# Norm steps and the gated output read from PSUM, transposes sharing banks, in a fused macaron layer

## The reference

```
x = x + 0.5 * ffn(layernorm(x))      # router argmax over 8 experts, hidden 512, relu
x = x + attention(layernorm(x))
x = x + 0.5 * ffn(layernorm(x))      # the same weights
```

```
q, k, v = silu(x @ Wq), silu(x @ Wk), silu(x @ Wv)
scores = (q k^T) * mask ; o = scores v + lam_q * (q @ kv) ; kv = lam_c * kv + (k * lam_k)^T v
o = (o - mean) * rsqrt(var + eps) * gamma + beta
out = o * sigmoid(x @ Wg1 @ Wg2) @ Wo
```

## Time and profile before

| | us |
|---|---|
| median of 3 runs | 478.96 (478.88 to 479.79) |
| profiled execution, its own time | 478.87 |
| its span | 476.9 |
| outside the span | 1.97 |
| DVE busy in the span | 333.1 (70%) |
| PE busy | 369.2 (77%) |
| POOL busy | 284.4 (60%) |

### The profile page before, as it was taken

One profiled execution on the slowest core, in us unless ns is written; L12 is line 12 of the kernel. 1 busy time (PEld: TensorE's weight loads), 2 busy tenths in 40 slices (PEclk: granted clock), 3 DMA queues, 4 the chain that ended last, 5 costly groups with the idle time before them and its releaser, 6 DMA issues.

```text
span 476.9 us, 10199 instructions
## 1 busy us (share of the span) xinstructions
PE 369.2 (77%) x2508; PEld 328.8 (69%) x2508; DVE 333.1 (70%) x957; ACT 195.3 (41%) x586; POOL 284.4 (60%) x292
## 2 busy tenths in 40 slices
PE   4967999999898683854859797885078999999940
PEld 4966889999786563643647677664068988999930
DVE  3593566444647999899968896989966568556520
ACT  2542744555363230515343526243035544555510
POOL 0007764737864769393875776670067776777771
PEclk9999999999999986796979897988568999999995
DMA  8627886887620000000110101010157774676610
GB/s 241 250 71 240 235 227 195 225 202 212 200 76 19 11 11 6 7 11 0 55 52 1 40 6 46 0 44 1 45 180 217 233 196 151 195 209 209 174 38 0
DMA packets 41303, 54.00 MB, mean 113 GB/s; under 512 B 6212, under 2 KB 25818, under 8 KB 40992
## 3 DMA queue, kind: packets, MB, share of 16 engines
q1 hardware_dynamic: 34496, 39.49, 26.8%
q0 software_dynamic: 6176, 13.26, 11.2%
q10 hardware_dynamic: 576, 0.62, 0.5%
HBM read 41.93 MB, written 12.32 MB: 114 GB/s over the span
## 4 chain that ended last, share of the span: by engine, by line
PE 40%; DVE 19%; issue 16%; POOL 16%; DMA 3%; ACT 2%; DVEq 1%; POOLq 0%; ACTq 0%
PE bank L1232 14%; PE bank L1222 13%; POOL outer_all L298 5%; POOL rows L401 4%; PE bank L1184 3%; PE bank L1282 3%; PE bank L1178 3%; PE bank L1316 2%; DVE st L716 2%; PE bank L1214 2%; POOL qS L458 2%; DMA const_sb<-in_const 1%; POOL out_x L420 1%; ACT o_n L541 1%; DVE hT_b L940 1%
## 5 line engine op out<-in xcount | busy, mean ns | idle before, releaser
L387 POOL DMA_INDIRECT ring<-rows_d,token_in x92 | 88.0, 957 | 99.1 <-DVE token_in L900 72.3
L1222 PE MATMUL bank<-slot_xT,w_ring 128*128 128x128 f32 x736 | 103.2, 282 | 6.1 <-DVE hT_b L940 5.3
L1222 PEld LDWEIGHTS bank<-slot_xT,w_ring 128*128 128x128 f32 x736 | 93.1, 196 | 9.4 <-DVE hT_b L940 7.3
L940 DVE TENSOR_SCALAR hT_b<-bank,b_cur 128x128 f32<-128x128 f32 x184 | 55.9, 345 | 38.3 <-PE bank L1222 31.1
L1282 PE MATMUL bank<-outer_all,decay_sb 128*128 128x256 f32 x256 | 72.8, 412 | 12.0 <-POOL outer_all L298 8.1
L1282 PEld LDWEIGHTS bank<-outer_all,decay_sb 128*128 128x128 f32 x256 | 50.6, 207 | 29.2 <-issue 9.1
L298 POOL TENSOR_TENSOR outer_all<-qkv 128x512 f32<-128x512 f32 x60 | 63.4, 1084 | 1.7 <-ACT qkv L610 1.6
L1232 PE MATMUL bank<-w_sb,hT_a 128*128 x368 | 60.5, 288 | 3.7 <-issue 0.7
L572 ACT ACTIVATE hT_a<-bank,b_cur 128x128 f32<-128x128 f32 x184 | 57.5, 364 | 12.2 <-PE bank L1222 11.3
L1232 PE MATMUL bank<-w_sb,hT_b 128*128 x368 | 56.8, 277 | 0.0
L991 DVE TENSOR_REDUCE o_in<-qS 128x64 f32<-128x256 f32 (+1 forms) x64 | 53.6, 856 | 3.5 <-POOL qS L458 3.5
(11 more groups left out here) (127 smaller groups left out, 579.6 us busy)
## 6 DMA issues: line engine op xcount, KB each, us to landing
w_ring<-in_w1t SPq DMA_DIRECT2D x92, 256.0 KB
rows_d<-rows SPq DMA_DIRECT2D x8, 512.0 KB, 3.0
y_d<-y_sb SPq DMA_DIRECT2D x46, 64.0 KB
rows<-in_x SPq DMA_DIRECT2D x8, 256.0 KB, 7.8
w_sb<-in_w2t SPq DMA_DIRECT2D x1, 2048.0 KB, 9.4
rows_d<-rows SPq DMA_DIRECT2D x8, 256.0 KB, 2.3
ring<-rows_d,token_in POOLq DMA_INDIRECT x92, 4.1
decay_sb<-in_decay SPq DMA_DIRECT2D x1, 1024.0 KB
```

Of the source, the lines that this page charges most:

```text
L387: pool.indirect_dma_start(n_in_ring(G) if layer_of(G) == 0 else in_ring(G), None, rows_d[u], bass.IndirectOffsetOnAxis(ap=token_in[u][:, j ...
L940: last = nc.vector.tensor_scalar(hT_b[G % 2][:, f * P:(f + 1) * P], bank_b[:, f * P:(f + 1) * P], b1_cur[G % 2][:, 2 + f:3 + f], 0.0, ALU. ...
L1222: last = mm(to[:, f * P:(f + 1) * P], w1_ring[G % W1_BUFS][:, (2 * half + f) * P:(2 * half + f + 1) * P], slot_xT[G % 2][:, :], start=True ...
```

## The change

The norm's small steps keep `mean2`, `var` and `tt` in the last columns of PSUM bank 5 instead of in SBUF, and are written so that no step has more than one input in SBUF. That takes one step more (`SMALL` is 12, i = 0 to 12) and 17 instructions instead of 14. `output_copy` writes its result back into bank 3, and `gate` reads it there. To free bank 5, the transpose of xn goes to bank 3 and the transpose of q to bank 6, with the waits that go with it. `front` moves ahead of the last two `sum_d`, and on ScalarE `gate_tanh` ahead of `route_copy`. `y_bank` is bank 7 in the first layer and stays bank 6 in the second.

```diff
-        mean2, var, yy, tt, uu = (sb(n, [P, LN_W]) for n in ("mean2", "var", "yy", "tt", "uu"))
+        spread2, gap, yy, uu = (sb(n, [P, LN_W]) for n in ("spread2", "gap", "yy", "uu"))
+        ln_bank = bank[5]
+        mean2, var, tt = (ln_bank[:, 512 - (i + 1) * LN_W:512 - i * LN_W] for i in range(3))
...
-        SMALL = 11
+        SMALL = 12
...
-                nc.scalar.activation(o_nT[:, :], bank[3][:, :], ACT.Identity, bias=gb_sb[:, 1:2],
+                nc.scalar.activation(bank[3][:, :], bank[3][:, :], ACT.Identity, bias=gb_sb[:, 1:2],
...
                 if i == 0:
-                    nc.vector.tensor_tensor(mean2[:, c], st[:, c, 1], st[:, c, 4], ALU.add)
-                    stt(out=var[:, c], in0=st[:, c, 2], scalar=D * EPS, in1=st[:, c, 5], op0=ALU.add, op1=ALU.add)
-                    ins = nc.vector.tensor_tensor(tt[:, c], st[:, c, 1], st[:, c, 4], ALU.subtract)
+                    nc.vector.tensor_reduce(var[:, c], st[:, c, 2::3], AX_X, ALU.add)
+                    ins = nc.vector.tensor_reduce(mean2[:, c], st[:, c, 1::3], AX_X, ALU.add)
                 elif i == 1:
-                    ins = nc.vector.tensor_tensor(uu[:, c], tt[:, c], tt[:, c], ALU.mult)
+                    nc.vector.tensor_scalar(spread2[:, c], var[:, c], D * EPS, None, ALU.add)
+                    stt(out=gap[:, c], in0=st[:, c, 1], scalar=2.0, in1=mean2[:, c], op0=ALU.mult, op1=ALU.subtract)
+                    ins = stt(out=tt[:, c], in0=st[:, c, 1], scalar=2.0, in1=mean2[:, c], op0=ALU.mult, op1=ALU.subtract)
...
                 elif i == 10:
+                    ins = stt(out=tt[:, c], in0=tt[:, c], scalar=-10 / 8 / ROOT_3_8, in1=uu[:, c], op0=ALU.add, op1=ALU.mult)
+                elif i == 11:
                     ins = stt(out=rstd[par][:, c], in0=tt[:, c], scalar=15 / 8, in1=yy[:, c], op0=ALU.add, op1=ALU.mult)
...
-                nc.vector.scalar_tensor_tensor(out=o_gT[:, :], in0=gateT[s.par][:, :], scalar=1.0, in1=o_nT[:, :],
+                nc.vector.scalar_tensor_tensor(out=o_gT[:, :], in0=gateT[s.par][:, :], scalar=1.0, in1=bank[3][:, :],
...
+                        if h == PAIRS - 2 and k + 1 < STEPS:
+                            front(step(k + 1))
                         sum_d(here, h)
-                if k + 1 < STEPS:
-                    front(step(k + 1))
...
             def carry_product(s):
                 pe.wait_ge(kd_done, s.n + 1)
-                pe.wait_ge(gate_done, s.n + 1)
+                pe.wait_ge(qdT_done, s.n + 2)
...
             def q_transpose(s):
                 pe.wait_ge(qkv_done, BATCH * (s.n + 1))
-                transpose4(bank[5], lambda b: qkv[s.par][:, b * 3 * D:b * 3 * D + D], qT_ready)
+                wait(pe, gate_done, s.n)
+                transpose4(bank[6], lambda b: qkv[s.par][:, b * 3 * D:b * 3 * D + D], qT_ready)
```

More of the change, by code:

```diff
@@ L273, in build @@
         ROUTE_TURN = SPLIT[1][0] - 1 + 3
-        xT_bank, bank_a, bank_b, y_bank = bank[0], bank[1], bank[2], bank[6]
+        xT_bank, bank_a, bank_b = bank[0], bank[1], bank[2]
+        y_bank = [bank[7], bank[6]]
         counts_bank = bank[5]
-        router_bank = [bank[4], bank[7]]
-        SMALL = 11
+        router_bank = [bank[4], bank[6]]
+        SMALL = 12
         halved_by = lambda n, h: sum(helped(m, j) for m in range(n + 1) for j in range(PAIRS) if (m, j) <= (n, h))
@@ L587, in attn_front @@
                 wait(act, gate_ready, s.n - 1)
-                nc.scalar.activation(xnT[s.par][:, :], bank[5][:, :], ACT.Copy).then_inc(xnT_copied, 1)
+                nc.scalar.activation(xnT[s.par][:, :], bank[3][:, :], ACT.Copy).then_inc(xnT_copied, 1)
                 if s.n >= 2:
@@ L604, in copy_first_xn @@
                 act.wait_ge(xnT_ready, 1)
-                nc.scalar.activation(xnT[0][:, :], bank[5][:, :], ACT.Copy).then_inc(xnT_copied, 1)
+                nc.scalar.activation(xnT[0][:, :], bank[3][:, :], ACT.Copy).then_inc(xnT_copied, 1)
             def first_qkv(first):
@@ L657, in attention @@
                     age_carry(k - 1)
+                if k >= 0:
+                    gate_tanh(step(k))
                 if 0 <= k - 3:
@@ L660, in attention @@
                 if k >= 0:
-                    gate_tanh(step(k))
                     act.wait_ge(ln_ready, ln_turn(k) + 1)
@@ L735, in small @@
                 elif i == 3:
+                    ins = stt(out=var[:, c], in0=spread2[:, c], scalar=4.0 / D, in1=tt[:, c], op0=ALU.mult, op1=ALU.add)
+                elif i == 4:
                     ins = nc.vector.tensor_scalar(yy[:, c].bitcast(I32), var[:, c].bitcast(I32), -0.5, RSQRT_MAGIC,
                                                   ALU.mult, ALU.add)
[L739 to L742, removed]
+                elif i in (5, 8):
+                    ins = nc.vector.tensor_tensor(tt[:, c], var[:, c], yy[:, c], ALU.mult)
@@ L952, in add_y @@
                         to = bias_ = x_in_ring(G)
-                    nc.vector.scalar_tensor_tensor(out=to, in0=y_bank[:, 0:D], scalar=0.5, in1=bias_,
+                    nc.vector.scalar_tensor_tensor(out=to, in0=y_bank[l][:, 0:D], scalar=0.5, in1=bias_,
                                                    op0=ALU.mult, op1=ALU.add).then_inc(y_done, 1)
@@ L971, in front @@
                 wait(dve, inter_ready, s.n - 1)
-                nc.vector.tensor_tensor(per_batch(qdT[s.par][:, :]), per_batch(bank[5][:, :]),
+                nc.vector.tensor_tensor(per_batch(qdT[s.par][:, :]), per_batch(bank[6][:, :]),
                                         cst("decay_q").unsqueeze(1).to_broadcast([P, BATCH, P]),
@@ L1090, in _ @@
             dve.wait_ge(wr_summed, 1)
-            nc.vector.tensor_copy(wr_sum[:, :], bank[6][:, 0:EXPERTS]).then_inc(wr_sum_copied, 1)
+            nc.vector.tensor_copy(wr_sum[:, :], bank[7][:, 0:EXPERTS]).then_inc(wr_sum_copied, 1)
             dve.wait_ge(const_loaded, 16)
@@ L1231, in down @@
                         h = (hT_a, hT_b)[f // 2][G % 2]
-                        last = mm(y_bank[:, 0:D], h[:, f % 2 * P:(f % 2 + 1) * P], w2_sb[:, bass.ds(expert[G] + f * D, D)],
+                        last = mm(y_bank[l][:, 0:D], h[:, f % 2 * P:(f % 2 + 1) * P], w2_sb[:, bass.ds(expert[G] + f * D, D)],
                                   start=(f == 0), stop=(f == FB - 1))
@@ L1250, in norm_transpose @@
                 pe.wait_ge(xn_done, BATCH * (s.n + 1))
-                wait(pe, qdT_done, s.n)
-                transpose4(bank[5], lambda b: xn[:, b * D:(b + 1) * D], xnT_ready)
+                wait(pe, gated, s.n - 2)
+                transpose4(bank[3], lambda b: xn[:, b * D:(b + 1) * D], xnT_ready)
             def project(s, b):
@@ L1367, in _ @@
                     pe.wait_ge(const_loaded, 16)
-                    mm(bank[6][:, 0:EXPERTS], cst("ones"), wr_sb[:, :], start=True, stop=True).then_inc(wr_summed, 1)
+                    mm(bank[7][:, 0:EXPERTS], cst("ones"), wr_sb[:, :], start=True, stop=True).then_inc(wr_summed, 1)
                 if r == SPLIT[0][0] + 1:
```

18 lines of the change are left out of this document (8 added, 10 removed).

## The result

The changed kernel takes 454.59 us (median of 4 runs, 452.03 to 455.7) against 479.38 (478.88 to 480.38): a ratio of 0.9473, 95% interval 0.9429 to 0.9517. In a second series of 6 runs, where the kernel before had 479.31, it took 457.85 (451.77 to 458.9), ratio 0.9531 (0.9483 to 0.9579). The longest of these six, 458.9, lies more than 1.5% above the shortest, counts as a slow run and is left out of the ratio. The forecast was 455.1.

What follows compares the result with a forecast made beforehand. Taken as the bound: the wait ending last in each stage, with VectorE's small steps stretched beside GpSimd. Saved 25.65 us less 1.85 lost gave net 23.8, from 478.87 to 455.1 us; range 447 to 466.

Steps and rivals of the forecast that it cites:

- What bounds, and the port: VectorE's small steps and gate: a second SBUF input waits for a port shared with GpSimd; all their stretching ends.
- Rival 2: Norm steps on VectorE: PSUM makes each cost up to twice its time, 463 to 465 us; chance 0.09.
- Loop B: GpSimd's work per turn: 19.0 us busy plus 2.6 of waits, 21.6 us, bounding turns 1 and 2 (22.5 in turn 1).
- GpSimd's wait at the head: Start of a full turn: GpSimd has 5.9 us of work until 8.1 us and so waits 2.2 us.
- Rival 5: GpSimd's stream fills every turn as before, so no gain shows though stretching ends; chance 0.01.
- Turns 4 to 6: VectorE and TensorE in series: 11.7 us plus a tail of 6.4 to 8.2, taken as 19.0 a turn, saving 7.85.
- the 20.5: Sign of being wrong: turns 4 to 6 taking over 20.5 us.
- PEclk nearer to 1: Sign of being right: TensorE's granted clock in turns 4 to 6 rises, with turns of 18 to 20 us.
- The wait at `carry_product`: TensorE's new wait for front: under 1.5 us, hidden because the transpose waits for ScalarE until 3.6 us anyway.
- The price without cover: TensorE's wait for front at carry_product, if no other wait hid it: 1.5 us a turn.
- Turns 3 and 7: Turn 3 keeps its 2.28 us DMA wait, takes 23.9 and saves 2.2; turn 7 loses 1.25 by the later shift.
- Ahead of the attention: First layer's norms: the second group loses 0.25 us by added small steps, the first group is hidden.

Runs made afterwards that it cites:

- e1: The changed kernel with mean2, var and tt back in SBUF, the same 17 instructions in the same places: 490.4 us, ratio 1.0232 to the kernel before.
- e2: The changed kernel with output_copy writing the SBUF tile o_nT again and the gate reading it there: 460.9 us, ratio 0.9587 to the kernel before.
- e4: The changed kernel with step 10 writing its result to SBUF, so that rstd alone has two SBUF inputs: 458.18 us, ratio 0.9588 to the kernel before.
- e5: The changed kernel with inter_product run twice, the same matmuls into the same bank again: 450.27 us, ratio 0.9416 to the kernel before.
- e7: The changed kernel with GpSimd's last add_back moved behind the first four of turn 3's outer products for the next turn: 446.44 us, ratio 0.9311.
- e8: The changed kernel with the edits of e5, e6 and e7 together: 445.03 us, ratio 0.9303 to the kernel before.
- e10: The changed kernel with front one sum_d earlier still, ahead of sum_d(5): 456.79 us, ratio 0.957 to the kernel before.
- e11: The changed kernel with the late add_back of e7 and the earlier front of e10 together: 452.94 us, ratio 0.9488 to the kernel before.
- e6: The changed kernel with steps 11 and 12 both ahead of sum_d(5), for an earlier shift: 453.46 us, ratio 0.9496 to the kernel before.
- e9: The kernel of e3 with inter_product run three times in place of once: 461.81 us, ratio 0.9652 to the kernel before.
- e3: The changed kernel with front behind the last sum_d again, carry_product still waiting for it: 475.58 us, ratio 0.9917 to the kernel before.

## Why the prediction was right, and where it was not

The total was within 0.5 us of the first series and 2.8 of the second; part of that was luck, since its terms erred on both sides: turns 4 to 6 brought 4.15 us less than forecast, turns 0 to 3 2.85 more, and the stages ahead of and behind them 2.25 more. From the profiled executions (476.9 - 452.1 = 24.8 us of span):

| | forecast | measured |
|---|---|---|
| ahead of turn 0's second `times_q` | -0.25 | 1.2 |
| turn 0 | 2.4 | 2.6 |
| turn 1 | 7.4 | 8.7 |
| turn 2 | 5.8 | 7.1 |
| turn 3 | 2.2 | 2.25 |
| turns 4 to 6 | 7.85 | 3.7 |
| turn 7 and behind | -1.6 | -0.8 |

**What bounds, and the port.** Right. The small steps now last 0.14 to 0.20 us beside GpSimd, the gate 0.68; e1, e2 and e4 bring the stretching back for just those instructions whose second input lies in SBUF. This agrees with the Trainium skill, page "SBUF — State Buffer", section "Who interferes with whom". Measurement adds how long: the 3.28 us of the gate and the 5.84 of the step end with a row of several GpSimd instructions, not with the first of them.

**Rival 2, dear writes to PSUM.** Next to nothing of it. `rstd`, which writes SBUF, has 169 ns for 12 elements; the steps L753 and L755, which write the bank, have 178 and 177: some 10 ns. The overhead of 125 against 60 ns in the Trainium skill, page "Perfetto Trace Analysis", section "Optimizing Scalar/DVE Operations", does not show: the serial part of turn 4 from the second `times_q` to the end of `shift` took 11.75 us (230.72 to 242.47) where the sum with no overhead was 11.7.

**Loop B.** The mechanism was right, the term too long by 1.3 us a turn (20.3 to 21.2 against 21.6 to 22.5). "The second `times_q` starts after 5.0 us" was read from a tail in which TensorE ran at 1.2 GHz; at the start of turns 2 and 3 it ran at 2.4, and the second `times_q` starts 3.4 us behind the start of `state_product(0)` (183.07 to 186.51, 203.41 to 206.84). GpSimd's wait at the head, forecast at 2.2 us, was 0.18 and 0.15. (Rival 5's "It idled 7.38 us per turn" is read too widely: that is the wait at the heads of turns 2 and 3; at the head of turn 1 it was 1.79.)

**Turns 4 to 6.** This step failed: "If TensorE keeps 2.4 GHz, the tail shrinks ... A turn then takes 18.1 to 19.9; I take the middle". Both levels occur, but the middle does not. A turn at 2.4 GHz takes 18.2 to 18.7 us (turn 4 here; all three in e5, e7, e8). Turns with a fall to 1.2 GHz took 21.9 and 20.9, here and in the second series (20.0 to 20.5 in e10 and e11, with a shorter fall), well over the 19.9, since the upper bound came from a tail of which only a part had run at the low level. That is also over the 20.5 which the prediction had named as a sign of being wrong. The tail was 6.6 us in turn 4 (forecast 6.4) and 9.8 in turn 5 (261.15 to 270.95). "PEclk nearer to 1" was wrong for turns 5 and 6, where it is 0.84; before it was 0.85 and 0.92.

**The wait at `carry_product`.** "The new wait thus lies under another one" was right as to time: the transpose behind it doesn't wait any more, and e10 shows the wait for ScalarE come out when `front` is earlier. The forecast laid the two only 0.1 us apart (3.5 and 3.6 us); e6 and e10 show them nearly level. The wait itself was 1.6 to 1.8 us, not under 1.5. The price without cover, 1.5 us a turn, held for the order (1.4 in e9), but left out the clock, which made e3 cost 5.6 in turn 4.

**Turns 3 and 7.** The DMA wait of 2.28 us stayed, as 1.92, and the turn is 23.88 against 23.9. In turn 7 `shift` starts 12.90 us behind the second `times_q` where it was 11.75: 1.15 later; the stage behind it gave some of that back.

**Ahead of the attention.** The 1.2 us there are not shown to be a gain. Over the kernels whose code ahead of it is the same, this point lies between 147.06 (e6) and 150.67 (e2), and the kernel before has 150.12. That, and turn 1 (21.2 us here, 22.8 with PEclk 0.78 in the second series), is most of what lies between the profiled executions of the two series.

**What stays open.** What decides, between turns alike, whether the clock falls. Waits of 1.6 to 1.8 us at `carry_product` were followed by 1.2 GHz in turns 5 and 6 here and by none in turn 4, nor in any of turns 3 to 6 of e7; in e4 turn 5 stayed at 2.4 GHz behind 2.15 us and turn 6 fell behind 2.10; in e2 turn 4 fell behind 1.61 us and turns 5 and 6 stayed behind 1.59 and 1.67. Shown is only that in turns 4 to 6 the clock stayed up where the stretch was filled (e5, e9), and that it fell where the stretch was split (e10, e11). Why an edit in turn 3 changed turns 5 and 6 was not tried by itself. The Trainium skill, page "TensorE: Matmul & The Clock Gate", section "Part 1: The HAM clock gate", says that what watches TensorE's activity runs on by itself and is not reset when a kernel starts. By that, equal waits at other moments may end differently; no run here shows whether this was the reason.

## What to carry to other kernels

Look for VectorE instructions with two SBUF inputs that last as long as a row of GpSimd's beside them; one input in PSUM ended that here, and writing there too cost some 10 ns a step. When such a stall goes, the next price can be TensorE's clock: cost each idle stretch of TensorE in two cases, once as a wait alone and once with what follows it at 1.2 GHz, and don't take their middle. A wait for a transfer ahead of work that others need can be worth moving even where it is short: 1.9 us of it, with the 1.3 us of addition behind it, cost 4.8 us in its turn.

## What was not expected of the hardware

- An added 1.8 us of TensorE work a turn made a kernel faster by 14 us (475.58 to 461.81), with PEclk at 1.00 in turns 4 to 6 where it was 0.79.
- The same matmul group, four of 128x256, takes 1.03 to 1.13 us or 2.05, with values such as 1.56 (e10) where the clock changed within it, and PEclk in windows of 1 us shows 1.00 or 0.50 with few values between.
- A two-input step of 12 elements stood for 5.84 us until a row of five GpSimd instructions was through.
- Waits of the same length were followed by both levels of TensorE's clock: 1.60 us in turn 4 by 2.4 GHz, 1.58 us in turn 6 by 1.2.
